# Graph network on one core: four node block numbers packed in one word, taken apart with register operations

## Chip, cores, metric

One Trainium2 chip, one of its cores. The metric is the device time of the program in microseconds (us), the median of three executions.

## What is computed

Two graph layers over 3125 nodes of 256 features and 50000 edges sorted by destination, each followed by a residual sum and a layer norm. The first (L0) is three hops of weighted neighbour sums with dense layers, the second (L1) is an attention layer with eight heads.

```python
edge_index = jnp.stack([src, dst])
x = _layernorm(x + L0(x, edge_weight, Wn, bn, Ws, bs, src, dst))
x = _layernorm(x + L1(x, W, a_src, a_dst, edge_W, edge_b, bias, edge_attr_3, edge_index))

# L0, three times
Hn = segment_sum(H[cols] * vals[:, None], rows, N) @ Wn[i].T + bn[i]
H = elu(Hn + H @ Ws[i].T + bs[i])          # no elu after the last

# L1
alpha = leaky(<h_src, a_src> + <h_dst, a_dst> + <relu(edge_attr @ edge_W.T + edge_b), h_dst>)
ex = exp(alpha - segment_max(alpha, dst)[dst])
attn = ex / segment_sum(ex, dst)[dst]
out = segment_sum(h_src * attn, dst)
```

## The kernel before

Every engine has an instruction sequence written out by hand, with counted semaphores between them; no scheduler moves anything. Nodes are cut into blocks of 128, called windows: 25 hold nodes, and their numbers run from 0 to 24 (NW = 26 counts one that stays empty). The stages, in order of time:

1. Edges are ranked and scattered by (source, destination) pair, and later by destination (GpSimd's indirect DMAs, L602, L612, L627).
2. Blocks of a dense adjacency matrix are summed by one-hot products on TensorE (L847) and merged on VectorE (L1570).
3. Three hops of dense products with those blocks (L909, L917). Beside the second hop VectorE and TensorE rank the edges by destination (the generator `side`). Its last step gives the window numbers: L1599 marks where each window begins among the chunks, a product sums the marks (L779), and L1602 takes one off and writes them as integers.
4. The score stage, 2141 to 2660 us. The edges now stand in 416 chunks of 128, all edges of a chunk with destinations in one window. Four chunks are a quad (104 of them), 16 a block (26). GpSimd gathers the source rows of every chunk (L641), TensorE looks up the destination rows by a one-hot product with the rows of the chunk's window (L988, `x0[:, bass.ds(ws[...], 1), :]`), ScalarE clips the encodings (L1186) and copies the gathered source terms (L1203), VectorE makes the scores (L1694, L1702, L1708).
5. The maxima and exponentials of the segments.
6. The summing stage, 2703 to 2975 us, in the loops `attend` (TensorE), `sum_chunks` (VectorE), `attend` (ScalarE) and `scale_rows` (GpSimd), each over the quads. GpSimd scales the rows of a quad (L657), ScalarE makes its one-hot matrices (L1225, L1231), TensorE sums each chunk in a PSUM bank (L1033; eight banks, two quads), and VectorE adds that bank to the accumulator of the chunk's window (L1835): even chunks to `acc`, odd ones to `x0`. TensorE waits for the add of chunk n before it writes chunk n + 8. VectorE runs a quad behind: in the part for quad g it takes the exponential columns of quad g + 2 (`exp_columns`, L1841) and adds quad g - 1.
7. Division, residual, layer norm, store.

In stages 4 and 6 the window's number must be in a register of the engine, since it is part of an address. The row `win_next` in SBUF holds one number of 32 bits for each chunk. `windows` (L406) emits one load for n consecutive numbers on the engine named. Eight at a time are loaded, in every second quad:

```python
if q % 2 == 0:
    ws = windows(mybir.EngineType.PE, win_next, 4 * g + 1, U)        # score, TensorE, L963
...
if q % 2 == 0:                                                       # sum_chunks, VectorE
    c = 1 + 4 * (g - 1)
    ws = windows(mybir.EngineType.DVE, win_next, c, U) if not (first and q == 0) else (
        (None,) * 4 + tuple(windows(mybir.EngineType.DVE, win_next, 1, 4)))
```

On VectorE blocks 1 to 24 are the 24 turns of a hardware loop (L1862); the first and the last block and the last quad are written out. Each add is L1831 (a register instruction for a semaphore value), L1833 (a wait), and L1835 (the address of the window, then the add itself).

Of the kernel before, what the change touches and what calls it, by code (L numbers as in the profile page):

```python
# [8 lines left out]
I32 = mybir.dt.int32  # L9
ALU = mybir.AluOpType  # L10
# [12 lines left out]
U = 8  # L23
NW = 26
USED = (N + P - 1) // P
# [33 lines left out]
NC = 416  # L59
NCD = NC + 16  # L60
NB = NC // 16
NQ = NC // 4
# [6 lines left out]
NA = 10  # L69
MID = 4  # L70
MIDWAY = 14
LOCAL = 9
SPLITS = 11
ROWS_STORED = 2 * (NG - 1)
assert (P - 1) * PAD_STEP + NS <= N
assert EC % PIECE == 0 and PIECE % 4 == 0 and 0 < LAST < EC and EC % U == 0 and SEGS * SEGC == EC and SEGS % 2 == 0 and SEGC % MID == 0
assert NS % U == 0 and HALF % (U // 2) == 0 and HALF < E // P and NS >= (P * EC + P * NBK) // P + 1
assert NC % 16 == 0 and NC % U == 0 and NC >= (E + USED * (P - 1)) // P
# [2 lines left out]
def build(nc, x, src, dst, edge_attr, edge_weight, Wn, bn, Ws, bs, W, a_src, a_dst, edge_W, edge_b, bias, out):  # L81
    with ExitStack() as ctx:
        def sb(name, shape, dt=F32, where=ctx):
            return where.enter_context(nc.sbuf_tensor(name, shape, dt))
# [33 lines left out]
        bias_b = sb("bias_b", [P, D])  # L118
        place = sb("place", [P, 2, EC], I32)
        block_row = sb("block_row", [1, NS + U], I32)  # L120
        win_next = sb("win_next", [1, NC + U], I32)
        rec = sb("rec", [P, NCD, REC])
        digits = sb("digits", [P, 2 * EC + 3 * MID * SEGS + 6 * DIG + 4 * 2 * HN])

# [11 lines left out]
        digit, q = carve(0, [EC, 2], BF16)  # L136
        rk, q = carve(q, [EC])
        rk_i, q = carve(q, [3, SEGS, MID], I32)
        begin, q = carve(q, [4, DIG])
# [98 lines left out]
        ends = sb("ends", [P, NB, 2])  # L238
        end_keys = sb("end_keys", [P, NB, 2])
        cin = sb("cin", [P, NB, 2])  # L240
        late = wT[:, :, :, :].rearrange("p m a o -> p (m a o)")
        er = late[:, 0:8 * HX].rearrange("p (s c d) -> p s c d", s=2, c=4)
        accf = acc[:, :, :].rearrange("p w d -> p (w d)")
# [159 lines left out]
        def nodes(t):  # L403
            return t.rearrange("(w p) d -> p w d", p=P)

        def windows(engine, row, c, n):  # L406
            return nc.values_load_multi_w_load_instructions(  # L407
                row[0:1, bass.ds(c, n)], engines=(engine,), min_val=0, max_val=NW - 1,
                skip_runtime_bounds_check_because="a count of the USED windows, less one")[1]

        def split(eng, parts, full, sem_, q):
            for i in range(3):
# [271 lines left out]
        def _(pe):  # L684
# [274 lines left out]
            def score(b, p0, first, second):  # L959
                for q in range(4):  # L960
                    g = 4 * b + q
                    if q % 2 == 0:
                        ws = windows(mybir.EngineType.PE, win_next, 4 * g + 1, U)  # L963
                    pe.wait_ge(s_ohT, g + 1)
                    los_row(g + 1, q + 1)
                    if q == 0 and not first and not second:
                        pe.wait_ge(s_alTs, b - 1)
                    pe.wait_ge(s_fst, b + 1 + (q + 1) // 4)
                    pe.wait_ge(s_eaTs, g + 1)
                    pe.nop(nofuse=True)  # L970
                    pe.transpose(bank[1][:, 0:P // 2].bitcast(BF16),
                                 fst[:, (p0 + (q + 1) // 4) % 2, 4 * ((q + 1) % 4):4 * ((q + 1) % 4) + 4, :]
                                 .rearrange("p c f -> p (c f)"), identb[:, :]).then_inc(s_eaT, 1)
                    for p in range(2):
                        n = 2 * g + p
                        if not (first and n < 2):
                            pe.wait_ge(s_relu, n - 1)
                        for c in range(2):
                            i = pe.matmul(bank[2 + p][:, c * D:(c + 1) * D], eaT[:, q % 2, :], ew_j[:, 2 * p + c, :],
                                          start=True, stop=True)  # L980
                        i.then_inc(s_enc, 1)
                    for p in range(2):
                        n = 2 * g + p
                        if not (first and n < 2):
                            pe.wait_ge(s_prod, n - 1)
                        for c in range(2):
                            j = 2 * p + c
                            i = pe.matmul(bank[4 + j][:, 0:HX], ohT[:, q % 2, j * P:(j + 1) * P],  # L988
                                          x0[:, bass.ds(ws[4 * (q % 2) + j], 1), :].rearrange("p c k -> p (c k)"),
                                          start=True, stop=True)  # L990
                        i.then_inc(s_hd_, 1)
                    if q == 3 and not first:
                        transpose_alpha(b - 1)
# [265 lines left out]
        def _(dve):  # L1259
# [328 lines left out]
            def dst_ranks():  # L1588
                dve.wait_ge(s_lowb, 16)
                v.tensor_scalar(place[:, 1, :], rec_i[:, 0:EC, 1], SHIFT - 1, None, ALU.logical_shift_right).then_inc(s_dg, 1)  # L1590
                dve.wait_ge(s_dg, LOW_END + 1)
                v.tensor_copy(digit, place[:, 1, :].unsqueeze(2).broadcast_to([P, EC, 2])).then_inc(s_dg, 1)
                dve.wait_ge(s_dg, DST0)
                yield from digit_ranks(1, NCD, 0, window_begins, DST0)
                yield
                dve.wait_ge(s_ex, 1)
                v.tensor_copy(ex_col[:, :], bank[6][0:HI, 0:1]).then_inc(s_exc, 1)
                dve.wait_ge(s_exc, 1)
                v.tensor_scalar(started[:, :], iota_f[0:HI, 0:NC], ex_col[:, 0:1], None, ALU.is_ge).then_inc(s_exc, 1)  # L1599
                yield  # L1600
                dve.wait_ge(s_ex, 2)
                v.tensor_scalar(win_next[:, 1:NC + 1], bank[7][0:1, 0:NC], -1.0, None, ALU.add).then_inc(s_exc, 1)  # L1602

            def split_features():
                dve.wait_ge(s_dback, 16)
# [224 lines left out]
            def add(n, k, w):  # L1830
                dve.wait_ge(s_mm, n + 1)  # L1831
                if not (isinstance(n, int) and n < 2):
                    dve.wait_ge(s_add, n - 1)  # L1833
                a = (acc, x0)[k % 2][:, bass.ds(w, 1), :].rearrange("p c d -> p (c d)")
                v.tensor_tensor(a, a, bank[k][:, 0:HX], ALU.add).then_inc(s_add, 1)  # L1835
# [8 lines left out]
            def sum_chunks(b, first, last):  # L1844
                for q in range(4):
                    g = 4 * b + q
                    if not (last and q >= 2):
                        exp_columns(g + 2, (q + 2) % 4, first and q < 2)
                    if q % 2 == 0:
                        c = 1 + 4 * (g - 1)  # L1850
                        ws = windows(mybir.EngineType.DVE, win_next, c, U) if not (first and q == 0) else (
                            (None,) * 4 + tuple(windows(mybir.EngineType.DVE, win_next, 1, 4)))
                    if not (first and q == 0):
                        for j in range(4):
                            add(4 * (g - 1) + j, 4 * ((q + 1) % 2) + j, ws[4 * (q % 2) + j])

            dve.wait_ge(s_exs, len(quads))
            exp_columns(0, 0, True)
# [3 lines left out]
            with dve.Fori(1, NB - 1) as b:  # L1862
                sum_chunks(b, False, False)
            sum_chunks(NB - 1, False, True)
            ws = windows(mybir.EngineType.DVE, win_next, 1 + NC - 4, 4)
            for j in range(4):
                add(NC - 4 + j, 4 + j, ws[j])

# [69 lines left out]
```

## Time and profile before

| | us |
|---|---|
| median of 3 executions | 3022.4 |
| lowest, highest | 3022.11, 3025.37 |
| profiled execution | 3022.19 |
| its span, first to last instruction | 3020.4 |
| TensorE busy | 2449.5 (81%) |
| VectorE busy | 1720.3 (57%) |
| ScalarE busy | 1068.3 (35%) |
| GpSimd busy | 1850.8 (61%) |
| granted TensorE clock, share of full | 0.928 |

### The profile page before, as it was taken

```text
span 3020.4 us, 46971 instructions
## 1 busy us (share of the span) xinstructions
PE 2449.5 (81%) x9398; PEld 1575.0 (52%) x9399; DVE 1720.3 (57%) x4277; ACT 1068.3 (35%) x3018; POOL 1850.8 (61%) x1739
## 2 busy tenths in 40 slices
PE   6999976477777779999899999999777677737772
PEld 5888853255555544445444454445555455525552
DVE  7765558899999940001344401113687777765557
ACT  1222221488888830000000000000233333347773
POOL 4777777777777770000057777770677777757774
PEclk9999999699999999999999999999788888869997
DMA  4000010355555564444344444543577777747672
GB/s 128 3 4 3 3 25 3 106 183 183 183 184 183 183 202 140 136 129 113 99 124 122 126 119 124 145 133 100 153 218 218 218 217 218 218 140 218 205 211 81
DMA packets 425651, 415.44 MB, mean 138 GB/s; under 512 B 85386, under 2 KB 411489, under 8 KB 424929
## 3 DMA queue, kind: packets, MB, share of 16 engines
q1 hardware_dynamic: 367681, 348.28, 37.1%
q0 software_dynamic: 57888, 66.23, 9.3%
q8 instruction: 32, 0.52, 0.1%
q14 instruction: 50, 0.41, 0.0%
HBM read 247.08 MB, written 167.17 MB: 137 GB/s over the span
## 4 chain that ended last, share of the span: by engine, by line
PE 50%; POOL 15%; issue 12%; SPq 10%; DVE 6%; DMA 4%; DVEq 2%; ACT 1%; ACTq 0%; POOLq 0%
PE psum L917 27%; POOL gath L641 10%; SPq L491 7%; PE psum L729 5%; POOL rows_by_pair L602 5%; PE psum L1033 4%; PE psum L714 3%; PE psum L909 2%; SPq L485 2%; DVEq L407 2%; DMA gath<-gat_rows,rec 1%; PE psum L788 1%; DMA adjacency<-merged 1%; PE psum L705 1%; PE psum L877 1%
## 5 line engine op out<-in xcount | busy, mean ns | idle before, releaser
L627 POOL DMA_INDIRECT rows_by_dst<-rec,place x392 | 381.5, 973 | 531.5 <-DVE place L1462 403.7
L917 PE MATMUL psum<-a_t,acc 128*128 128x512 f32 (+1 forms) x1400 | 553.7, 551 | 0.0
L641 POOL DMA_INDIRECT gath<-gat_rows,rec x416 | 403.4, 970 | 214.7 <-issue 119.0
L612 POOL DMA_INDIRECT rows_by_low_digit<-rec,place x392 | 440.5, 1124 | 128.2 <-issue 128.2
L847 PE MATMUL psum<-rhot,lw 128*128 128x256 f32 x1440 | 383.6, 420 | 158.1 <-ACT lw L1104 130.9
L602 POOL DMA_INDIRECT rows_by_pair<-rec,place x392 | 385.9, 984 | 160.6 <-issue 127.1
L847 PEld LDWEIGHTS psum<-rhot,lw 128*128 128x128 f32 x1440 | 277.5, 207 | 264.3 <-ACT lw L1104 168.7
L917 PEld LDWEIGHTS psum<-a_t,acc 128*128 128x128 f32 x1400 | 257.3, 195 | 272.1 <-issue 268.3
L1570 DVE SCALAR_TENSOR_TENSOR merged<-merged,same_of,psum 128x256 f32<-128x256 f32 x720 | 310.0, 477 | 31.3 <-PE psum L847 17.4
L917 PE MATMUL psum<-a_t,x 128*128 128x512 f32 (+1 forms) x700 | 294.2, 548 | 0.0
L1104 ACT ACTIVATE lw<-lhot,recs_pair 128x128 f32<-128x128 bf16 x720 | 236.8, 388 | 95.2 <-DVE lhot L1553 81.2
L988 PE MATMUL psum<-x,acc 128*128 x832 | 258.8, 459 | 4.6 <-DVE acc L1702 4.4
L1033 PE MATMUL psum<-ht 128*128 128x264 f32 x832 | 200.3, 394 | 70.3 <-DVE acc L1835 66.6
L657 POOL TENSOR_TENSOR ht<-gath,digits 128x1024 f32<-128x1024 f32 x104 | 196.5, 1912 | 74.2 <-PE psum L1033 66.3
L1033 PEld LDWEIGHTS psum<-ht 128*128 128x128 f32 x832 | 154.2, 191 | 116.2 <-DVE acc L1835 87.6
L729 PEld LDWEIGHTS psum<-table,ohhiT 32*128 32x128 f32 x784 | 181.1, 318 | 53.5 <-issue 32.0
L988 PEld LDWEIGHTS psum<-x,acc 128*128 128x128 f32 x832 | 180.6, 231 | 50.2 <-issue 16.4
L729 PE MATMUL psum<-table,ohhiT 32*128 32x16 f32 x784 | 202.2, 375 | 1.7 <-ACT table L1064 1.7
L1646 DVE TENSOR_SCALAR et<-et 128x512 f32<-128x512 f32 (+1 forms) x28 | 11.0, 394 | 335.2 <-ACT et L1132 334.6
L1702 DVE TENSOR_TENSOR acc<-wT,psum 128x528 f32<-128x528 f32 x208 | 145.2, 698 | 92.3 <-issue 39.4
L917 PEld LDWEIGHTS psum<-a_t,x 128*128 128x128 f32 x700 | 126.2, 191 | 114.0 <-issue 108.9
L1339 DVE SCALAR_TENSOR_TENSOR terms<-psum,kst,earlier 128x128 f32<-128x128 f32 (+1 forms) x392 | 140.0, 413 | 44.8 <-PE psum L714 34.3
(320 smaller groups left out, 3397.8 us busy)
## 6 DMA issues: line engine op xcount, KB each, us to landing
a_t<-adjacency SPq DMA_DIRECT2D x450, 256.0 KB, 2.7
adjacency<-merged SPq DMA_DIRECT2D x721, 128.0 KB
gat_h_by_edge<-gath SPq DMA_DIRECT2D x104, 528.0 KB, 4.2
gath<-gat_h_by_edge SPq DMA_DIRECT2D x104, 528.0 KB, 4.1
gath<-gat_rows,rec POOLq DMA_INDIRECT x416
rows_by_pair<-rec,place POOLq DMA_INDIRECT x392
rows_by_low_digit<-rec,place POOLq DMA_INDIRECT x392
rows_by_dst<-rec,place POOLq DMA_INDIRECT x392
```

What stands on the lines that cost most here:

```text
L491: sp.dma_start(adj[bass.ds(to[j], 1), :, :].rearrange("b p c -> p (b c)"), merged[:, j, :]).then_inc(s_st[j], 16)
L602: pool.indirect_dma_start(out=rows_pair, in_=rec[:, c, :], out_offset=bass.IndirectOffsetOnAxis(ap=place[:, 0, c:c + 1], axis=0), in_offse ...
L612: pool.indirect_dma_start(out=rows_low, in_=rec[:, c, :], out_offset=bass.IndirectOffsetOnAxis(ap=place[:, 1, c:c + 1], axis=0), in_offset ...
L627: pool.indirect_dma_start(out=rows_dst, in_=rec[:, c, :], out_offset=bass.IndirectOffsetOnAxis(ap=place[:, 0, c:c + 1], axis=0), in_offset ...
L641: pool.indirect_dma_start(out=gath[:, g % 4, c % 4, :], out_offset=None, in_=hh_dram, in_offset=bass.IndirectOffsetOnAxis(ap=rec_i[:, c, 0 ...
L729: pe.matmul(bank[7 * s][:, j * LO:(j + 1) * LO], ohhiT[:, 4 * s + j, :], table[:, half, :], start=True, stop=True, skip_group_check=True). ...
L847: pe.matmul(bank[j % 4][:, 0:SW], lw[:, p, j, :], rhot[:, p, j, :], start=True, stop=True).then_inc(s_bmm, 1)
L917: i = pe.matmul(sums[b], table_g[:, w, b * P:(b + 1) * P], a_t[:, q % NA, 0:width(g)], start=False, stop=w == USED - 1)
L988: i = pe.matmul(bank[4 + j][:, 0:HX], ohT[:, q % 2, j * P:(j + 1) * P], x0[:, bass.ds(ws[4 * (q % 2) + j], 1), :].rearrange("p c k -> p (c ...
L1033: pe.matmul(bank[4 * (q % 2) + j][:, 0:HX], onehot[:, q // 2, 4 * (q % 2) + j, :], val[:, q, j, :], start=True, stop=True).then_inc(s_mm, 1)
L1104: nc.scalar.activation(lw[:, p, j, :], lhot[:, p, j, :], ACT.Copy, scale=recs_pair[:, bass.ds(at, 1), 2]).then_inc(s_lw, 1)
L1570: v.scalar_tensor_tensor(out=merged[:, j, :], in0=merged[:, (j - 2) % U, :], scalar=same_of[:, bass.ds(s, 1)], in1=bank[j % 4][:, 0:SW], o ...
```

## The change

The row of one number per chunk goes. Behind L1602 three small VectorE instructions pack the numbers of four chunks into one word, five bits each, chunk 0 lowest, with multiply-adds in fp32 (20 bits are exact there): `quad_windows` has 104 words. The unpacked row and the intermediate ones stand in space that the ranking used. `windows` loads n words and takes each apart with shifts and masks in registers. VectorE loads one word in every quad; TensorE two words in every second quad.

```diff
+WBITS = 5
+assert USED <= 1 << WBITS and 4 * WBITS <= 24
...
-        win_next = sb("win_next", [1, NC + U], I32)
+        quad_windows = sb("quad_windows", [1, NQ], I32)
...
+        window_row = picked[0:1, :, :, :].rearrange("p b g s -> p (b g s)")[:, 0:2 * NC].rearrange("p (r c) -> p r c", r=2)
...
-        def windows(engine, row, c, n):
-            return nc.values_load_multi_w_load_instructions(
-                row[0:1, bass.ds(c, n)], engines=(engine,), min_val=0, max_val=NW - 1,
-                skip_runtime_bounds_check_because="a count of the USED windows, less one")[1]
+        def windows(engine, g, n=1):
+            words = nc.values_load_multi_w_load_instructions(
+                quad_windows[0:1, bass.ds(g, n)], engines=(engine,), min_val=0, max_val=(1 << 4 * WBITS) - 1,
+                skip_runtime_bounds_check_because="four counts of the USED windows, less one, of WBITS bits each")[1]
+            eng = {mybir.EngineType.PE: nc.tensor, mybir.EngineType.DVE: nc.vector}[engine]
+            return [eng.compute_val((word >> WBITS * j) & (1 << WBITS) - 1).with_bounds(min_val=0, max_val=NW - 1)
+                    for word in words for j in range(4)]
...
                     if q % 2 == 0:
-                        ws = windows(mybir.EngineType.PE, win_next, 4 * g + 1, U)
+                        ws = windows(mybir.EngineType.PE, g, 2)
...
-                v.tensor_scalar(win_next[:, 1:NC + 1], bank[7][0:1, 0:NC], -1.0, None, ALU.add).then_inc(s_exc, 1)
+                v.tensor_scalar(window_row[:, 0, :], bank[7][0:1, 0:NC], -1.0, None, ALU.add).then_inc(s_exc, 1)
+                of = [window_row[:, 0, :].rearrange("p (g j) -> p j g", j=4)[:, j, :] for j in range(4)]
+                word = window_row[:, 1, :].rearrange("p (j g) -> p j g", j=4)
+                for j, (high, low, to) in enumerate(((of[3], of[2], word[:, 0, :]), (word[:, 0, :], of[1], word[:, 1, :]),
+                                                     (word[:, 1, :], of[0], quad_windows[:, :]))):
+                    dve.wait_ge(s_exc, j + 3)
+                    v.scalar_tensor_tensor(out=to, in0=high, scalar=float(1 << WBITS), in1=low, op0=ALU.mult,
+                                           op1=ALU.add).then_inc(s_exc, 1)
...
-                    if q % 2 == 0:
-                        c = 1 + 4 * (g - 1)
-                        ws = windows(mybir.EngineType.DVE, win_next, c, U) if not (first and q == 0) else (
-                            (None,) * 4 + tuple(windows(mybir.EngineType.DVE, win_next, 1, 4)))
                     if not (first and q == 0):
+                        ws = windows(mybir.EngineType.DVE, g - 1)
                         for j in range(4):
-                            add(4 * (g - 1) + j, 4 * ((q + 1) % 2) + j, ws[4 * (q % 2) + j])
+                            add(4 * (g - 1) + j, 4 * ((q + 1) % 2) + j, ws[j])
...
-            ws = windows(mybir.EngineType.DVE, win_next, 1 + NC - 4, 4)
+            ws = windows(mybir.EngineType.DVE, NQ - 1)
```

```order
L1840 REGISTER_ALU
L1841 ISA
L1841 TENSOR_REDUCE ht<-digits 128x4x8
L1831 REGISTER_ALU
L1833 REGISTER_ALU
L1835 ISA
L1835 TENSOR_TENSOR acc<-acc,psum 128x264
L1831 REGISTER_ALU
L1835 ISA
L1835 TENSOR_TENSOR x<-x,psum 128x264
```

Changed:

```order
L1853 REGISTER_ALU
L1854 ISA
L1854 TENSOR_REDUCE ht<-digits 128x4x8
L410 REGISTER_ALU
L410 TENSOR_LOAD quad_windows
L414 REGISTER_ALU x7
L1844 REGISTER_ALU
L1846 REGISTER_ALU
L1848 ISA
L1848 TENSOR_TENSOR acc<-acc,psum 128x264
```

Nine sequencer instructions now stand between the reduction and the first add of this quad that were not there. All four quads of a turn have this form. In a quad that had a load (q = 0 and 2) the load changes its size, and the seven of L414 and one L1844 are new.

TensorE at the head of a turn of its loop in the score stage. Before:

```order
L407 REGISTER_ALU
L407 TENSOR_LOAD win_next
L964 REGISTER_ALU
L955 ISA
L955 MATMUL psum<-identb,lo_b 128x128
```

Changed:

```order
L410 TENSOR_LOAD quad_windows
L414 REGISTER_ALU x14
L970 REGISTER_ALU
L961 ISA
L961 MATMUL psum<-identb,lo_b 128x128
```

The load stands where it stood, with fourteen register instructions behind it.

## Rows read from the trace of the kernel before

**Rows 1.** The page's part 4, the chain that ended last, by line.
```profile
PE psum L917 27%; POOL gath L641 10%; SPq L491 7%; PE psum L729 5%; POOL rows_by_pair L602 5%; PE psum L1033 4%; PE psum L714 3%; PE psum L909 2%; SPq L485 2%; DVEq L407 2%; DMA gath<-gat_rows,rec 1%; PE psum L788 1%; DMA adjacency<-merged 1%; PE psum L705 1%; PE psum L877 1%
```

**Rows 2.** Summing stage: length, busy PE, PEld, DVE, ACT, POOL, clock, DMA share, GB/s.
```profile
2706.00:2972.00 266.00, 199.28 (x829) 153.70 (x830) 157.47 (x509) 199.62 (x513) 193.60 (x103) 0.99 0.69 203
```

**Rows 3.** VectorE in order of time, one turn of its loop (start us, us, instruction).
```profile
2784.60 0.43 DVE L1835 TENSOR_TENSOR acc<-acc,psum 128x264 f32 x1 [1.91 <-PE psum L1033]
...
2785.63 0.42 DVE L1835 TENSOR_TENSOR x<-x,psum 128x264 f32 x1
...
2786.06 0.42 DVE L1835 TENSOR_TENSOR acc<-acc,psum 128x264 f32 x1
...
2789.89 0.43 DVE L1835 TENSOR_TENSOR acc<-acc,psum 128x264 f32 x1 [2.02 <-PE psum L1033]
...
2790.92 0.42 DVE L1835 TENSOR_TENSOR x<-x,psum 128x264 f32 x1
...
2791.55 0.43 DVE L1835 TENSOR_TENSOR acc<-acc,psum 128x264 f32 x1
...
2792.58 0.42 DVE L1835 TENSOR_TENSOR x<-x,psum 128x264 f32 x1
...
2794.99 0.43 DVE L1835 TENSOR_TENSOR acc<-acc,psum 128x264 f32 x1 [1.89 <-PE psum L1033]
```

**Rows 4.** TensorE in the same stretch, in order of time.
```profile
2785.09 3.83 PE L1033 MATMUL psum<-ht 128*128 128x264 f32 x16 [1.28 <-DVE acc L1835]
```

**Rows 5.** The chain of waits from 2787 to 2796 us.
```profile
2787.80 1.85 DVEq L407
2789.65 0.05 issue
...
2792.91 0.19 DVEq L407
...
2794.80 0.04 DVEq L1833
...
2794.89 0.06 DVEq L1835
```

**Rows 6.** Who waited for whom in the summing stage (total us, times, longest).
```profile
PE psum L1033 <- DVE acc L1835: 66.6, 50, 1.5
```

**Rows 7.** Loads into registers (duration ns min/median/max): L407, its first and last on VectorE, SyncE's.
```profile
L407 DVEq TENSOR_LOAD <-win_next x53: 961/1846/1861, 2703.0 to 2972.8; - x53
L407 PEldq TENSOR_LOAD <-win_next x52: 1936/2469/3076, 2141.2 to 2644.8; - x52
...
L407 DVEq TENSOR_LOAD <-win_next x1: 1215/1215/1215, 2703.0 to 2703.0; - x1
...
L407 DVEq TENSOR_LOAD <-win_next x1: 961/961/961, 2972.8 to 2972.8; - x1
...
L493 SPq TENSOR_LOAD <-block_row x1: 282/282/282, 1099.7 to 1099.7; - x1
...
L485 SPq TENSOR_LOAD <-block_row x90: 737/758/798, 560.5 to 1094.1; - x90
```

**Rows 8.** The score stage: chain by line, busy times, ScalarE's waits, a gather.
```profile
by line: POOL gath L641 58.7%; issue 25.1%; DMA gath<-gat_rows,rec 8.7%; PE psum L988 3.5%; PE psum L979 0.7%; ACT digits L1203 0.6%; PE psum L955 0.6%; DVE acc L1702 0.4%; ACTq L1203 0.2%; DVE ht L1734 0.2%; DVE ht L1728 0.2%; DVE ht L1731
...
2160.00:2660.00 500.00, 353.75 (x1730) 259.27 (x1729) 384.76 (x672) 168.34 (x528) 379.52 (x396) 0.84 0.74 218
...
ACT digits L1203 <- DMA gath<-gat_rows,rec: 262.7, 92, 4.5
...
2191.55 0.95 POOL L641 DMA_INDIRECT gath<-gat_rows,rec  x1 [0.30 <-ACT digits L1203]
```

**Rows 9.** VectorE's first add of the summing stage.
```profile
2707.51 0.43 DVE L1835 TENSOR_TENSOR acc<-acc,psum 128x264 f32 x1 [3.05 <-PE psum L1033]
```

**Rows 10.** VectorE around the window numbers, second hop.
```profile
1761.56 0.57 DVE L1602 TENSOR_SCALAR win_next<-psum 1x416 int32<-1x416 f32 x1
1773.68 0.39 DVE L1646 TENSOR_SCALAR et<-et 128x53 f32<-128x53 f32 x2 [11.55 <-ACT et L1132]
```

## The prediction

> **What bounds the kernel now.** I read the chain that ended last first, by line [rows 1]: the largest part, 27%, are the hops (L917), where no number is loaded. The change touches only places that load window numbers. They are two: the score stage on TensorE, and the summing stage on VectorE (the stage from 2706 to 2972 us), whose loads stand there as "DVEq L407 2%".
>
> In the summing stage no engine is full [rows 2]: of 266 us PE is busy 199, POOL 194, ACT 200, VectorE 157. Four quads make one turn of the VectorE loop (L1862), and the turn takes 10.39 us, from the add at 2784.60 to the one at 2794.99 [rows 3]. One turn holds 16 adds 0.34 apart, 4 reductions, and two holes of 2.02 and 1.89 us. The profile names TensorE as what ended the holes. That is not so: the matmuls of these adds were done earlier, since TensorE stopped at 2785.09 + 3.83 = 2788.92 [rows 4] and the add comes at 2789.89. What fills the hole is in the chain of waits [rows 5]: the load of eight window numbers runs from 2787.80 for 1.85 us, then come two register instructions and the add. TensorE waits in turn for that add (66.6 us in 50 waits [rows 6]), since chunk n + 8 uses chunk n's bank, and POOL and ACT for TensorE. So VectorE's instruction sequence sets the pace of all: its loads and register work are on the path at full length. The 266 us hold 25.6 turns, so in a turn PE works 7.8 us, POOL 7.6, ACT 7.8, all under 10.39.
>
> In the score stage TensorE also stops for loads (52 of eight words, median 2.47 us [rows 7]). But there 58.7% of the chain is POOL's gather and 25.1% "issue", mostly between gathers: each takes 0.95 us with 0.30 before it, 416 of them one after the other, and the 0.30 is the same where ACT is named as what ended it [rows 8].
>
> **The change, part by part.** Per turn of the VectorE loop the listing shows: 2 loads of eight words become 4 of one word; 28 register instructions are added to take the words apart; 2 address instructions for the added loads; 2 more at L1844 (the quads that used to load skip it). That is 32 register instructions more.
>
> *Loads gone.* 2 x 1.846, the median of the loads on VectorE, = 3.69 us [rows 7].
>
> *Loads added.* No VectorE load of one word is in the trace. VectorE's last load has four words and takes 0.96 us; eight take 1.85 [rows 7]. The line through both (0.961 and 1.847) is 0.075 + 0.2215 per word, so 0.30 for one: an estimate. Lower end: 0.23, an eighth of 1.85 (all cost goes by words). Upper end: the first load, also of four words, took 1.215, 0.25 more than the last; so 0.55. SyncE's one-word load took 0.282 beside 0.758 for eight, another line with nearly the same end at one word, which is why I take 0.30. Four of them: 1.20. From a load's end to the next instruction is 0.05 [rows 5]; two more of that: 0.10.
>
> *Register instructions.* L1833's record is only 0.04 us. What counts is the distance to the next one: it starts at 2794.80, L1835 at 2794.89, so 0.09 [rows 5]. Lower end: 0.04, if several in a row follow each other without the gap. Upper end: 0.113, a third of the 0.34 between two adds, which holds three sequencer instructions (L1831, L1833, L1835). I take 0.09, a direct distance: 32 x 0.09 = 2.88.
>
> *Are they covered?* An add is handed over as it starts, so the sequencer goes on while the last add of a quad and the reduction still run: the load at 2792.91 starts beside the last add, 2792.58 + 0.42 [rows 3, 5]. This cover is in the row already, and the load and unpacking come behind it. The next add cannot be handed over first, as its address comes out of them. So nothing covers them.
>
> *Sum of a turn:* 2.88 + 1.20 + 0.10 - 3.69 = +0.49 us; the loop has 24 turns: **+11.8**.
>
> *Outside the loop.* Each quad now costs 0.30 + 0.05 + 7 x 0.09 = 0.98. First block: the load before quad 0 was hidden, and the new one is too, since the first add waits 3.05 us for TensorE's first chunk [rows 9]; then 2 x 0.98 against 1.86 + 0.05: +0.05. Last block and last quad: 5 x 0.98 = 4.90 against 2 x 1.90 + 0.96 + 0.05 = 4.81: +0.09. Together +0.1.
>
> *Packing.* Three instructions of 1 x 104 behind L1602, itself 0.57 us. At 0.57 each or less they end by 1764; VectorE's next instruction waits for ACT until 1773.68, idle for 11.55 us [rows 10]. Nothing. Were the cover gone, 1.7 us at most.
>
> *TensorE in the score stage.* It loads two words for a pair of quads and runs 14 register instructions more. The load has no record of two words: between 0.5 (a quarter of the shortest of eight, 1.94) and 3.1. At 0.04 to 0.12 each the 14 are 0.5 to 1.7. So from 1.5 us less to 2.3 more than the median load, in a pair that POOL's gathers make some 8 x 1.26 = 10.1 us long. In 500 us of the stage TensorE is busy 354, its 50 loads take another 124, and ACT waits 262.7 us in 92 waits for gathered rows to land, 2.9 in each [rows 8]: what is scored is ahead of what is gathered by that much in every quad, 5.7 in a pair. Nothing on the path, either way. Were this cover gone, the upper end would cost 50 x 2.3 = 115 us.
>
> Against the profiled execution of 3022.2 us (span 3020.4), 0.2 under the median of 3022.4: 3022.2 + 11.8 + 0.1 = **3034 us**. A measurement tells about 0.2%, 6 us, from no change; this is 0.4%.
>
> One rule of the Trainium skill speaks for the change: Perfetto Trace Analysis, on DVE and ACT instructions, says that the sequencer is ready for the next instruction as soon as it has pushed one into the wait queue. By it register work would run beside the adds. The row shows how far that goes here: one add ahead. What the rule would make of the time is the third rival.
>
> **The rivals.**
>
> *Words are all that counts (same).* A load costs 0.23 a word, no fixed part: 4 x 0.07 less in a turn, +0.21 x 24 + 0.1: 3027. For it: eight words cost nearly twice four. Against: that leaves out the 1.215.
>
> *Register instructions in a row are cheap (faster).* Place: the seven behind each load. Price: 0.04 each, the recorded duration, so 32 x 0.04 = 1.28 in place of 2.88 and the turn is 1.11 us shorter than now: 3022.2 - 26.6 + 0.1 = 2996. It decides from 0.075 downwards: 32 x 0.075 + 1.30 = 3.70. For it: no row shows seven plain ones in a row. Against: the 0.05 stands behind the load as well as behind L1833 [rows 5].
>
> *They hide under the adds (faster).* With all 28 covered, 2.52 us a turn: 3034 - 60 = 2974. Against: the load itself was hidden by no more than 0.2 us, and it is the same sequencer.
>
> *Dearer pieces (slower still).* Loads at 0.55: +1.00 in a turn, 3034 + 24 = 3058. Or register instructions at 0.113: 32 x 0.023 = +0.74, 3034 + 17.7 = 3052. For it: at the turn's start and in its third gap the sequencer stands still longer than its instructions explain (2790.92 to 2791.55 is 0.63, the like gap from 2785.63 to 2786.06 is 0.43 [rows 3]), and the loop gets 34 instructions longer.
>
> *Another engine hides the difference.* PE, POOL and ACT need less than 8 us for a turn of 10.4, so this is unlikely: 3022.
>
> **How the numbers follow.** Forecast 0.58; words alone 0.17 and another engine 0.04, which are "same"; dearer pieces 0.14; cheap in a row 0.05, hidden 0.02. Slower: 0.58 + 0.14 = 0.72; same 0.21; faster 0.07. The forecast's own spread, with load and register price each a little off, is 3029 to 3042. The range takes in the same-cases with some room and the nearer half of the dear ones: 3018 to 3050. It leaves out the two faster rivals (0.07) and the far half of the dear ones (0.07).
>
> **What would show it.** Right: 104 VectorE loads of about 0.30 us; in the loop one hole of about 1.2 us before every quad in place of 2.0 before every second, and 10.9 us per turn; the summing stage 278 us; score stage, hops and tail unchanged. TensorE's score-stage loads shorter without the gathers' 1.257 moving. Wrong: adds of a turn that still start 0.44 apart across a quad's edge (hidden), the first add 0.4 us or less behind the load's end (cheap in a row), loads of over 0.5, or a changed time between two gathers.

## The result and the profile after

The changed kernel takes 3016.52 us (median of 14 runs, 3014.58 to 3018.97), the kernel before 3024.32 in the same comparison (14 runs, 3021.91 to 3025.37). The ratio is 0.9976, 95% interval 0.9967 to 0.9984: faster by 0.24%, 7.8 us. The prediction was 3034, slower by 0.4%, with a range from 3018; the result lies outside it, 1.5 us below its end, and has the other sign.

| us | before | after |
|---|---|---|
| profiled execution / its span | 3022.19 / 3020.4 | 3018.76 / 3016.7 |
| summing stage, first reduction to final add | 272.48 | 265.64 |
| one turn of VectorE's loop (median of 23) | 10.389 | 10.107 |
| score stage, first to last gather | 529.39 | 530.57 |

The summing stage has lost 6.84 us, and 24 turns x 0.28 = 6.8 is all of it. The profiled execution shows only 3.4, since its earlier stages ended 3.2 us later than those of the profiled execution before, in the scatters and gathers; the medians, 7.8 us apart, do not have that. The loads and the register instructions, from the lists of lines L410 and L414 (duration in ns: lowest/median/highest):

```profile
L410 DVEq TENSOR_LOAD <-quad_windows x104: 300/304/557, 2706.2 to 2969.3; - x104
L410 PEldq TENSOR_LOAD <-quad_windows x52: 537/1128/1640, 2143.0 to 2647.1; - x52
...
L414 PEldq ALU_OP x728: 32/36/41, 2143.8 to 2650.1; - x182
L414 DVEq ALU_OP x728: 40/45/57, 2706.8 to 2970.1; - x182
```

They answer to [rows 7]. A one-word load on VectorE is 0.30 us, as estimated, and the 728 unpacking instructions (7 for each of 104 quads) are all there. VectorE in order of time, one turn, the counterpart of [rows 3]:

```profile
2780.51 0.43 DVE L1848 TENSOR_TENSOR acc<-acc,psum 128x264 f32 x1 [1.06 <-PE psum L1039]
...
2783.00 0.43 DVE L1848 TENSOR_TENSOR acc<-acc,psum 128x264 f32 x1 [0.95 <-PE psum L1039]
...
2785.47 0.43 DVE L1848 TENSOR_TENSOR acc<-acc,psum 128x264 f32 x1 [0.93 <-PE psum L1039]
...
2787.87 0.43 DVE L1848 TENSOR_TENSOR acc<-acc,psum 128x264 f32 x1 [0.85 <-PE psum L1039]
...
2788.89 0.42 DVE L1848 TENSOR_TENSOR x<-x,psum 128x264 f32 x1
2789.39 0.19 DVE L1854 TENSOR_REDUCE ht<-digits 128x32 f32 x1
2790.63 0.43 DVE L1848 TENSOR_TENSOR acc<-acc,psum 128x264 f32 x1 [1.05 <-PE psum L1039]
```

The shape is the predicted one, a hole of about one microsecond ahead of every quad in place of two ahead of every second. But the turn is 2790.63 - 2780.51 = 10.12, where 10.9 was predicted and 10.39 was before. The chain of waits through one hole says why (start, us, what; "issue" is time between the records):

```profile
2792.30 0.04 DVEq L414
2792.35 0.03 issue
2792.38 0.04 DVEq L414
2792.42 0.03 issue
2792.45 0.04 DVEq L414
...
2792.75 0.04 DVEq L414
2792.79 0.03 issue
2792.82 0.04 DVEq L1844
2792.87 0.05 issue
2792.91 0.04 DVEq L1846
```

Seven unpacking instructions run from 2792.30 to 2792.82: 0.52 / 7 = 0.074 each. The 0.09 of the prediction is there too, from 2792.82 to 2792.91, but only where the next instruction carries a semaphore wait (L1846), and L1833 with L1835 behind it in [rows 5] was such a pair.

Elsewhere: in the score stage a gather still takes 1.26 us with its 0.30,

```profile
2190.95 0.95 POOL L647 DMA_INDIRECT gath<-gat_rows,rec  x1 [0.30 <-issue]
2192.21 0.95 POOL L647 DMA_INDIRECT gath<-gat_rows,rec  x1 [0.30 <-issue]
```

as in [rows 8]; and the packing lies in VectorE's idle time ahead of ScalarE's next result, as in [rows 10], with 10.38 us of it left:

```profile
1763.37 0.57 DVE L1608 TENSOR_SCALAR digits<-psum 1x416 f32<-1x416 f32 x1
1763.97 0.76 DVE L1614 SCALAR_TENSOR_TENSOR digits<-digits 1x104 f32<-1x104 f32 x2
1764.77 0.34 DVE L1614 SCALAR_TENSOR_TENSOR quad_windows<-digits 1x104 int32<-1x104 f32 x1
1775.49 0.39 DVE L1659 TENSOR_SCALAR et<-et 128x53 f32<-128x53 f32 x2 [10.38 <-ACT et L1138]
```

The terms of the prediction's sum, per turn, with what they measured:

| term | predicted | measured |
|---|---|---|
| two loads of eight words gone | -3.69 | -3.69 |
| four loads of one word | +1.20 | 4 x 0.304 = +1.22 |
| gaps behind loads | +0.10 | 4 x 0.034 - 2 x 0.05 = +0.04 |
| 28 unpacking instructions | +2.52 | 28 x 0.074 = +2.07 |
| two address instructions more | +0.18 | 4 x 0.072 - 2 x 0.092 = +0.10 |
| two instructions at L1844 | +0.18 | 2 x 0.088 = +0.18 |
| sum of these | +0.49 | -0.08 |
| the turn as it is | | -0.28 |

(0.034 and 0.072 are the distances from a load's end to the next start and from an address instruction to its load; the address calculation before was a fused one, 0.092 ahead of its load.) So the terms alone come to zero within what a run can tell, and 0.2 us per turn are none of them. Two places hold it. In before, from the last add of a turn across the branch to the next reduction:

```profile
2787.08 0.42 DVE L1835 TENSOR_TENSOR x<-x,psum 128x264 f32 x1
2787.69 0.19 DVE L1841 TENSOR_REDUCE ht<-digits 128x32 f32 x1 [0.18 <-PE psum L1033]
```

that is 0.61, and after 2788.89 to 2789.39, 0.50: the instruction behind the branch starts 0.19 after it instead of 0.29. And the longer gap that the prediction had noted (0.63 against 0.43 in the like one, [rows 3]) has lost its standstill. Of those 0.20 us 0.08 is one register instruction more (L1840), which the prediction did not take off, and 0.12 is time without an instruction: L1833 starts 0.21 behind L1831, where it is 0.09 in the like gap. The two like gaps of the change are 1.455 and 1.361, only 0.09 apart, and the same instruction (L1853 now) is most of that.

### The profile page after: what moved, and what is told of

Same layout as the page of the kernel before. It is cut to its first block, busy times and chain, and to the rows that moved or that the text cites. A ratio compares the mean times of both kernels' runs of the same rounds, so it can differ in the third digit from the quotient of the medians.

```text
span 3016.7 us, 48565 instructions
## 1 busy us (share of the span) xinstructions
PE 2460.3 (82%) x9398; PEld 1569.3 (52%) x9399; DVE 1722.3 (57%) x4280; ACT 1073.7 (36%) x3018; POOL 1855.6 (62%) x1739
## 4 chain that ended last, share of the span: by engine, by line
PE 37%; POOL 23%; issue 15%; SPq 10%; DVE 6%; DMA 4%; DVEq 3%; ACT 1%; ACTq 0%; POOLq 0%
PE psum L923 27%; POOL rows_by_pair L608 13%; POOL gath L647 10%; SPq L497 7%; PE psum L1039 2%; PE psum L915 2%; DMA gath<-gat_rows,rec 2%; SPq L491 2%; PE psum L794 1%; DMA adjacency<-merged 1%; PE psum L883 1%; PE psum L853 1%; DVE acc L1848 1%; DVEq L414 1%; DVE x L1848 1%
## 5 line engine op out<-in xcount | busy, mean ns | idle before, releaser
L1039 PE MATMUL psum<-ht 128*128 128x264 f32 x832 | 214.2, 402 | 48.8 <-DVE acc L1848 45.2
```

Source lines behind the costliest of these rows:

```text
L1039: pe.matmul(bank[4 * (q % 2) + j][:, 0:HX], onehot[:, q // 2, 4 * (q % 2) + j, :], val[:, q, j, :], start=True, stop=True).then_inc(s_mm, 1)
```

## The experiments

Two theories at first: A, VectorE's sequencer sets the pace of the summing stage, and a register instruction there costs its 0.074 on the path; B, the gain comes from TensorE's shorter loads. The two chips of the experiments e1 to e4 and e5 to e8 took 4268 and 4264 us for the kernel before, since the stages with scatters and gathers were longer there (first to last gather 694 to 705 us in place of 529), while VectorE's old loop has a turn of 10.38 there too (e2); ratios of those runs are of that longer time. "Turn" is the median over VectorE's loop, and a gap is from the start of the last add of a quad to the first of the next, in the order first, second, third and fourth quad of a turn. Before: 2.81, 0.63, 2.42, 0.44; after: 1.74, 1.46, 1.45, 1.36.

### One engine at a time

```diff
# e1: VectorE as changed; TensorE keeps its row of numbers
-                        ws = windows(mybir.EngineType.PE, win_next, 4 * g + 1, U)
+                        ws = windows8(mybir.EngineType.PE, win_next, 4 * g + 1, U)
...
# e2: TensorE as changed; VectorE keeps its loads of eight
```

> VectorE loads one packed word per quad as in the change; TensorE loads eight numbers per pair of quads as before (both tables are made, one more small VectorE instruction in the second hop). Theory A, the gain is VectorE's sequencer in the summing stage (turn of four quads 10.11 us, was 10.39; 24 turns): same time as the change, 3016 to 3018, turn 10.11, stage 265.6 us. Theory B, the gain is TensorE's shorter loads in the score stage: 3024, since its loads are eight words again.

> The reverse: TensorE loads two packed words, VectorE eight numbers as before. Theory A: time of before, 3024, turn 10.39, stage 272.5, gathers unchanged at 529 to 531 us from the first to the last. Theory B: 3017.

e1: 4260.59, ratio 0.9974 (0.9965 to 0.9983), turn 10.101. e2: 4269.59, ratio 1.0000 (0.9992 to 1.0009), turn 10.382. All of the effect is VectorE's; theory B falls, and that TensorE's part is hidden behind the gathers stands. The gathers were slower on that chip, which makes hiding easier; on the faster one it is the unchanged 1.26 us from gather to gather that speaks for it.

### More and fewer register instructions

```diff
# e3: seven masks more per load, which change nothing
+            if engine == mybir.EngineType.DVE:
+                for k in range(7):
+                    words = [eng.compute_val(word & (1 << 21 + k % 2) - 1) for word in words]
...
# e4: one mask in place of seven instructions
+            if engine == mybir.EngineType.DVE:
+                return [eng.compute_val(word & (1 << WBITS) - 1).with_bounds(min_val=0, max_val=NW - 1) for word in words] * 4
```

e4 leaves out the unpacking on VectorE: all four chunks of a quad are added to the first one's block.

> The change with seven more plain register instructions (masks that change nothing) behind every VectorE load. Theory A with the price that the trace of the change shows, 0.074 us each and nothing hidden: each of the four gaps 0.52 longer, turn 10.11 + 2.07 = 12.18, total 3016.5 + 103 x 0.52 = 3070. At the 0.09 of the prediction: turn 12.63, 3081. If most register work lay under the adds: turn under 11, under 3040.

> Leaves out the unpacking on VectorE: all four chunks of a quad are added to the block of the first one (one mask instead of seven register instructions). Theory A: six register instructions fewer in a quad, 0.44 us, turn 10.11 - 1.78 = 8.33, total 3016.5 - 46 = 2971. If another engine takes over on the way (ScalarE and TensorE are busy 7.8 us in a turn), the turn stays above 8.33 and the total above 2971.

e3: 4316.16, ratio 1.0115 (1.0099 to 1.0131). Its turn in the trace:

```profile
4000.37 0.43 DVE L1851 TENSOR_TENSOR acc<-acc,psum 128x264 f32 x1 [1.53 <-PE psum L1042]
...
4003.34 0.43 DVE L1851 TENSOR_TENSOR acc<-acc,psum 128x264 f32 x1 [1.42 <-PE psum L1042]
...
4012.62 0.43 DVE L1851 TENSOR_TENSOR acc<-acc,psum 128x264 f32 x1 [1.53 <-PE psum L1042]
```

12.25 long, median 12.26: 28 instructions cost 2.15, 0.077 each. In the second and third gaps (1.94, 1.93) seven cost 0.48 to 0.49, 0.069 each; in the first and the fourth (2.35, 1.94) 0.61 and 0.58. The rest has its place in the trace: the step behind the branch is 0.32 instead of 0.19, and in the fourth gap L410 comes 0.25 behind L1857 instead of 0.16. e4: 4214.08, ratio 0.9874 (0.9857 to 0.9891), turn 8.13. The 24 instructions less are 24 x 0.074 = 1.78, which gives the expected 8.33. The other 0.2 has two parts. The edit took more than the unpacking: as two adds of a quad now share an address, the trace has no address instruction ahead of the third and fourth, and the sequencer comes to each gap 0.11 sooner, 0.43 per turn. Against that the step behind the branch is 0.29 again, 0.10 more, and the second gap has a standstill of 0.12 (L410 comes 0.28 behind L1856, where it is 0.16 in the other gaps). 10.11 - 1.78 - 0.43 + 0.22 = 8.12. So the price is right, and it is on the path one for one; nothing else holds the stage down to 8.1 us per turn.

### Just ahead of its add

```diff
# e5; take() is the shift and the mask of one number
-                        ws = windows(mybir.EngineType.DVE, g - 1)
+                        word = windows(mybir.EngineType.DVE, g - 1)[0]
                         for j in range(4):
-                            add(4 * (g - 1) + j, 4 * ((q + 1) % 2) + j, ws[j])
+                            add(4 * (g - 1) + j, 4 * ((q + 1) % 2) + j, take(mybir.EngineType.DVE, word, j))
```

> The change, with each of VectorE's four numbers taken out of the word just ahead of its own add (one register instruction ahead of the first add, two ahead of each of the others) in place of all seven ahead of the first. Theory A (VectorE's sequencer paces the stage; between two adds of a quad, 0.34 us, its own instructions fill only about 0.285, and it waits 0.055 for the add before): two more register instructions of 0.074 between two adds use that slack, so a quad gets 3 x 0.055 = 0.165 us shorter, a turn 0.66 (10.11 to 9.45), the stage 16 us, ratio to the kernel before 0.992 where the change has 0.9976. Rival S (the sequencer has no slack: register instructions cost their 0.074 wherever they stand): turn 10.11, ratio 0.9976. Rival H (register instructions run beside an add altogether): six of seven hidden, 6 x 0.074 x 4 = 1.8 us per turn, turn 8.3.

e5: 4248.16, ratio 0.9963 (0.9952 to 0.9974); turn 9.667, stage 253.67 against 265.64.

```profile
3997.36 0.43 DVE L1852 TENSOR_TENSOR acc<-acc,psum 128x264 f32 x1 [0.53 <-PE psum L1043]
3997.80 0.43 DVE L1852 TENSOR_TENSOR x<-x,psum 128x264 f32 x1
3998.23 0.43 DVE L1852 TENSOR_TENSOR acc<-acc,psum 128x264 f32 x1
3998.67 0.43 DVE L1852 TENSOR_TENSOR x<-x,psum 128x264 f32 x1
3999.64 0.43 DVE L1852 TENSOR_TENSOR acc<-acc,psum 128x264 f32 x1 [0.44 <-PE psum L1043]
```

Adds are now 0.438 apart instead of 0.342 (mean of the three steps of a quad), so two instructions of 0.148 together cost 0.096 there: 0.052 of each pair is hidden, about the 0.055 of theory A. Over a quad that is 0.156 of which 0.11 arrived (0.44 per turn, where 0.66 was expected), because the gaps fell by 0.40 in place of 6 x 0.074 = 0.44. The rivals are out: S had 10.11, H 8.3. The prediction had cited the Trainium skill, Perfetto Trace Analysis, on DVE and ACT instructions, that the sequencer is ready for its next instruction once one is pushed into the wait queue. This trace agrees in kind: register instructions do run beside an add, but only 0.05 us of them per add, since each add with its wait and address needs 0.285 of the 0.34 (0.285 + 0.148 = 0.433, nearly the 0.438). In the change the sequencer stands inside a quad only ahead of L1846, the wait for an earlier add, by 0.07 and 0.05 us in two of the three places; in e5 both are gone, and their sum, 0.12 per quad, is about the 0.11 that arrived.

### Fewer instructions and fewer loads

```diff
# e6: beside e5
+            part = word >> WBITS * j if j == 3 else (word >> WBITS * j) & (1 << WBITS) - 1
...
+                    if q % 2 == 0:
+                        two = windows(mybir.EngineType.DVE, g - 1, 2) if not (first and q == 0) else [None, *windows(mybir.EngineType.DVE, 0)]
...
# e12: as e6, but one load of four words per turn
+                    if q == 0:
+                        four = windows(mybir.EngineType.DVE, g - 1, 4) if not first else [None, *windows(mybir.EngineType.DVE, 0, 3)]
```

> As the run before, and also no mask on the topmost field (one register instruction fewer per quad) and one load of two words for two quads in place of two loads of one. By the line through the measured loads (0.30 for one word, 0.96 for four) two words take 0.52, so a pair saves 0.08 and one address instruction and the gap behind the load, 0.1, together about 0.18 a pair; the mask gone saves 0.074 a quad at most, and 0 where the slack of the sequencer hid it already. Turn 9.45 - 0.36 - 0.30 = 8.8 at best, 9.1 if the mask was hidden; stage 24 to 33 us under the change's, ratio 0.987 to 0.990. Rival (two words cost two loads, 0.60): 0.36 smaller gain, ratio about 0.992.

e6: 4234.26, ratio 0.9922 (0.9906 to 0.9939), turn 9.07, stage 238.58; the load of two words takes 0.525. Against e5 the turn is 0.60 shorter. The mask came through in full: the four adds of a quad span 1.222 instead of 1.314, 0.37 per turn. The loads and what goes with them are 2 x (0.608 - 0.525) + 2 x 0.106 = 0.38. Another 0.07 comes from the sequencer's reaching each of the four gaps 0.017 sooner. Of these 0.82 the turn's start gives back 0.22: the step behind the branch is 0.29 again (e5: 0.19), and L410 comes 0.28 behind L1859 (e5: 0.16). The rival, two words at the price of two loads, is out by the record of 0.525.

> As e6_lean, with one load of four words per turn in place of two of two words: 0.965 in place of 2 x 0.525, and one address instruction (0.07) and one gap behind a load (0.03) fewer: 0.19 less, turn 9.07 - 0.19 = 8.88. The gap ahead of the first quad grows by 0.44 (1.77 to 2.21), the one ahead of the third falls by 0.63 (1.26 to 0.62). Against the kernel before the stage is then 24 x (10.39 - 8.88) = 36 us shorter plus about 2 outside the loop: 38 us, ratio 0.987 where the kernel before takes 3020 us, 0.991 where it takes 4265. Rival (something else paces a turn below 9 us, as TensorE with about 8 us of work in a turn, or POOL, or ACT): turn 9.07 or near it, and new idle time ahead of adds inside a quad.

e12: 2981.52 us beside 3022.38 for the kernel before, ratio **0.9863 (0.9845 to 0.9880)**; turn 8.89 against the expected 8.88, stage 234.24. It beats both kernels: 41 us under the one before, where the change as made gains 8. The load of four words and the adds around it, first from the list of line L410, then in order of time:

```profile
L410 DVEq TENSOR_LOAD <-quad_windows x27: 315/966/1004, 2703.7 to 2935.7; - x27
```

```profile
2786.52 0.42 DVE L1853 TENSOR_TENSOR x<-x,psum 128x264 f32 x1
2788.72 0.43 DVE L1853 TENSOR_TENSOR acc<-acc,psum 128x264 f32 x1 [1.38 <-PE psum L1044]
...
2789.94 0.42 DVE L1853 TENSOR_TENSOR x<-x,psum 128x264 f32 x1
2790.56 0.43 DVE L1853 TENSOR_TENSOR acc<-acc,psum 128x264 f32 x1
```

One gap of 2.2 per turn is left, and three of 0.54 to 0.63 with no idle time shown ahead of the add.

### The price of loads

```diff
# e7: the kernel before, a load of four numbers in every quad
+                        ws = windows(mybir.EngineType.DVE, win_next, 1 + 4 * (g - 1), 4)
```

> The kernel before, with one load of four words for every quad in place of one of eight for two; nothing is packed. If a load costs 0.08 and 0.22 per word (one word 0.30, four 0.96, eight 1.85): 4 x 0.96 + 0.1 in place of 2 x 1.85 in a turn, and two address instructions and two gaps more (about 0.25): turn 10.39 + 0.15 + 0.25 = 10.8, the stage +10 us, ratio 1.002. If only words count (0.231 each): turn 10.39 + 0.25 = 10.6. If a load costs more than that beside its words (the first load's 1.215): 4 x 0.25 more, turn 11.8, ratio 1.008.

e7: 4272.06, ratio 1.0015 (1.0003 to 1.0028), turn 10.655. The list of line L407 shows what a load costs:

```profile
L407 DVEq TENSOR_LOAD <-win_next x104: 959/965/1220, 3948.0 to 4224.0; - x104
```

Loads follow the line of the prediction: 0.075 + 0.2215 per word gives 0.297, 0.518, 0.961 and 1.847 for one, two, four and eight words, measured 0.304, 0.525, 0.965 and 1.846. The turn came out 0.15 under my sum all the same, nearer to the 10.6 of the rival in which only words count; that rival falls by the load itself, 0.965 where it had 0.924. The loads are +0.17 as worked out (4 x 0.965 - 3.69), and the two more address instructions and gaps are 0.28, but a quad that loads skips L1831, and two of these less are 0.18: my sum had left that out. The 1.215 of the first load in before belongs to the first load alone: it takes about 0.25 more than the later ones of its size in before (1.215 and 0.961), in the change (0.557 and 0.304) and in e7 (1.220 and 0.965). Why is not shown.

### The 0.2 us that no instruction explains

```diff
# e8: the kernel before, four masks more behind each of the loop's loads
+                        if not (first or last):
+                            for k in range(4):
+                                ws[0] = nc.vector.compute_val(ws[0] & (1 << 21 + k % 2) - 1).with_bounds(min_val=0, max_val=NW - 1)
...
# e9, e10: the kernel before, 3 and 8 such masks once, ahead of the loop; e11: 4 of them ahead of the loop of the change
+                        if first and q == 2:
+                            for k in range(3):
```

> The kernel before, with four more plain register instructions behind each load of eight words in VectorE's loop (8 in a turn), which change no number. At 0.074 each, the distance seen in the change: +0.59, turn 10.98; at the predicted 0.09: +0.72, turn 11.11. Each of the two gaps with a load grows by 0.30. The standstill of 0.12 us in the gap ahead of the turn's second quad (0.63, where 0.43 is explained by its instructions): if it belongs to that place in the program whatever stands ahead of it, it stays and the gap is 0.63; if it belongs to how the instructions lie one behind the other in the loop, it moves or goes with 8 more of them (the gap 0.5, and another one longer).

> The kernel before with three plain register instructions added once, ahead of VectorE's summing loop; the loop's own instructions are the same, each only stands three places later in the program. Theory P (the two standstills of the loop, 0.12 us in the gap ahead of the second quad and 0.1 at the branch back, depend on where the loop's instructions lie in the program): turn leaves 10.39; it lands between 10.1 and 10.4, and the step behind the branch, 0.29 from the branch to the next instruction, takes another value. Rival Q (they belong to what the loop does, waits and order of its instructions): turn 10.39, gaps 2.81 0.63 2.42 0.44, step behind the branch 0.29.

> As the run before, with eight register instructions ahead of the loop in place of three. Theory P: a turn of another length than 10.39 or than that of the run before, all three within 10.1 to 10.4. Rival Q: 10.39.

> The change with four plain register instructions added once, ahead of VectorE's summing loop. Theory P: the turn of 10.11 was a favourable place, so it gets longer or stays: 10.1 to 10.35, with the step behind the branch (0.19 in the change) at another value. Rival Q: 10.11, gaps 1.74 1.46 1.45 1.36, step behind the branch 0.19.

These four were one run each, and the turns are what they are for. e8 (4285.88 us): turn 10.957, eight instructions for 0.568, 0.071 each; gaps 3.10, 0.63, 2.71, 0.43, so the second gap keeps its length. e9 (3020.14 us): turn 10.388, and every gap as before. e10 (3022.28 us): turn 10.329, the second gap 0.56 in place of 0.63, in the trace

```profile
2791.97 0.43 DVE L1835 TENSOR_TENSOR x<-x,psum 128x264 f32 x1
2792.53 0.43 DVE L1835 TENSOR_TENSOR acc<-acc,psum 128x264 f32 x1
```

and the other gaps as before. e11 (3015.68 us): turn 10.106, as in the change. The lengths of the gaps hide what the starts of the sequencer's instructions show. One step of the turn is 0.12 longer than the same step elsewhere, and it is another one in each run:

| run | instructions put in ahead | step that is 0.12 longer | its length, and its usual one |
|---|---|---|---|
| before | 0 | L1831 to L1833, second gap | 0.21, 0.09 |
| e9 | 3 | L1840 to L1841, second gap | 0.21, 0.09 |
| e8 | 4 (in the loop, behind the first load) | L1835 to L1840, second gap | 0.24, 0.13 |
| e10 | 8 | L1835 to L1831, ahead of the quad's fourth add, before the second gap | 0.24, 0.13 |

Counted along the program (the reduction and the add count too), the step moves back by 3, 4 and 8 instructions when as many are put in ahead of it: the standstill stays at one place of the program, and other instructions come to lie there. So theory P holds for it and Q falls. In e10 it lies between adds, where 0.05 of it costs nothing, and the turn is 0.07 shorter.

P does not hold for the step behind the branch, which was 0.29 in e8, e9 and e10 as in before, and 0.19 in e11 as in the change. That step was 0.29 in loops of six different contents (before, e4, e6, e7, e8, e12), 0.19 in the change, e1 and e5, and 0.32 in e3. But the two go together: the four traces with 0.19 (the change, e1, e5, e11) show no such standstill in any step of the turn, and the other ten show one (0.12, in e3 0.09). The four have 94 sequencer instructions in a turn, the others 60 to 82 or 122 (e3). What sets either of them stays open.

## Why the prediction was wrong

- **What bounds the kernel: right.** VectorE's instruction sequence sets the pace of the summing stage. e1 and e2 separate it from TensorE; e3, e4 and e8 change the number of register instructions and the turn follows at 0.07 to 0.08 for each, once e4's missing address instructions are taken off.
- **The load of one word, 0.30: right** (0.304), and the line behind it holds at two and four words (e6, e7, e12). "Words are all that counts" falls.
- **The failed step is the price of a register instruction, "I take 0.09, a direct distance".** It was direct, but between L1833 and L1835, the second of which waits on a semaphore. Plain ones in a row are 0.074 apart. 28 x 0.016 = 0.45 per turn is 10.8 us of the predicted loss of 11.9. The rival "cheap in a row" had the direction and put its point of decision at 0.075; its own price, 0.04, was twice as far off on the other side. I gave it 0.05 because the rows had no plain pair, when a case with its threshold in the middle of my bounds (0.04 to 0.113) needed more.
- **Smaller terms of the same kind** were too dear as well: gaps behind loads (0.04, not 0.10) and address instructions (0.10, not 0.18). Together 0.14 per turn, 3.4 us.
- **The two standstills were noted and not followed.** They stood in the prediction as a reason for "dearer pieces", to grow with the loop; in the change the one of 0.12 is gone and the other 0.10 shorter. They are 0.2 us of the measured 0.28, so without them the change would be at -0.08 x 24 = -1.9 us, within 0.2% of before: by its instructions alone the change is "same", and the measured "faster" is mostly 24 x 0.2 = 4.8 us that no instruction accounts for. No line of the prediction foresaw this way to "faster". The 0.12 depends on what stands at one place of the program (e8, e9, e10); why the changed loop has none, and the shorter step behind its branch, is not shown.
- **Nothing covers the register work: right**, as it stands in the change (e3, e4: the turn follows it one for one). e5 shows how it could be covered, 0.05 per add.
- **Packing costs nothing; TensorE's loads in the score stage are hidden: right** (e2, ratio 1.0000).
- The range took in the "same" cases with 4 us of room and stopped there, though my lower bound for the register instruction's price led further down; a low end by 0.07 for each, 24 x 32 x 0.02 = 15 us under the forecast, 3019, and the standstills with it, 3014, would have held the result.

## What to carry to other kernels

On an engine whose sequencer is the pace, price a register instruction by the instruction that follows it, and where the sum is a difference of two large terms (3.69 against 4.18 here), work out the price at which its sign turns and give the sides chances by where the bounds lie around it. Do not stop at a trade that breaks even: with register work placed between the adds, where it is partly free, one load per turn and no needless mask, the same packing gained 41 us in place of 8. Differences of 0.1 us per turn of a loop can come from where its instructions stand, so a gain of that size should be looked for in the trace before it is put down to an edit; the starts of the sequencer's instructions show it, where the gaps between the adds can look unchanged.

## What was new about the chip in these runs

- On VectorE's sequencer a plain register instruction takes 0.074 us start to start (0.069 for the masks of e3 and e8), and 0.087 to 0.093 where the next one carries a wait; the record shows 0.04 for both.
- A load from SBUF into VectorE's registers takes 0.08 us and 0.22 more per word, from one word to eight (0.304, 0.525, 0.965, 1.846), and the first of the stage 0.25 on top.
- Between two adds 0.34 apart the sequencer has about 0.05 us to give (e5).
- A loop can hold a standstill of 0.12 us that stays at one place of the program while the loop's instructions are shifted past it (before, e8, e9, e10), so one gap of the same loop was 0.63 or 0.56 us. The step behind a loop's branch was 0.19, 0.29 or 0.32 us in different kernels, and 0.12 after the last turn, where the branch is not taken.
